# A decoder layer in one program: another buffer for the substitution's diagonal copy, another order around each group's boundary, and two engines that copy the solved rows

## The reference

```
def delta_rule(q, k, v, beta):                       # chunks of CS = 32 rows
    ...
    A = jnp.where(strict_lo, kb @ jnp.swapaxes(k, -1, -2), 0.0)
    Tinv = solve_triangular(eye + A, eye, lower=True, unit_diagonal=True)
    u = Tinv @ v
    w = Tinv @ kb
...
o = o * rsqrt(mean(o * o, -1) + 1e-05) * o_norm_w    # x = x + o @ o_proj_w.T
...
att = softmax(where(mask, q @ k.T / sqrt(16), -1e9))  # q from layernorm(x), k and v from the context
```

## Time and profile before

| | |
|---|---|
| median of 3 runs | 1211.49 us (1210.48 to 1219.17) |
| the profiled execution's own time | 1214.59 us |
| its span, from the first to the last instruction | 1212.8 us |
| mean granted clock of TensorE | 0.923 of full speed |
| busy share of the span | PE 85%, PEld 63%, DVE 68%, POOL 50%, ACT 44% |
| turns i = 0 to 7 of the loop, as stretches | 244.5 to 1004.0 us |

### The profile page before, as it was taken

One profiled execution on the slowest core, in us unless ns is written; L12 is line 12 of the kernel. 1 busy time (PEld: TensorE's weight loads), 2 busy tenths in 40 slices (PEclk: granted clock), 3 DMA queues, 4 the chain that ended last, 5 costly groups with the idle time before them and its releaser, 6 DMA issues.

```text
span 1212.8 us, 25582 instructions
## 1 busy us (share of the span) xinstructions
PE 1036.3 (85%) x9234; PEld 768.9 (63%) x9234; DVE 819.9 (68%) x2164; ACT 538.5 (44%) x1008; POOL 602.4 (50%) x998
## 2 busy tenths in 40 slices
PE   4899979486899899889989989979998898989982
PEld 2555558465677566666666656757666667767881
DVE  2989976834666756856766685684776765657576
ACT  3868754323334333432442433343243244754761
POOL 6877825147137346616806734651683124335552
PEclk9999999669799799989979989997998999999996
DMA  8365451530101511230161161121012064323588
GB/s 187 115 192 158 120 179 42 188 101 27 61 2 45 172 47 33 94 112 32 61 173 36 47 174 40 35 95 39 28 61 71 23 221 147 101 80 121 169 283 300
DMA packets 86796, 127.67 MB, mean 105 GB/s; under 512 B 28305, under 2 KB 62609, under 8 KB 84497
## 3 DMA queue, kind: packets, MB, share of 16 engines
q1 hardware_dynamic: 79472, 106.30, 29.1%
q0 software_dynamic: 7200, 19.74, 4.5%
HBM read 66.47 MB, written 59.55 MB: 104 GB/s over the span
## 4 chain that ended last, share of the span: by engine, by line
PE 44%; POOL 23%; DVE 16%; issue 8%; ACT 5%; DMA 3%; SPq 1%; ACTq 0%; DVEq 0%; POOLq 0%
POOL arena L1519 7%; POOL arena L1521 6%; PE bank L551 3%; PE bank L511 3%; POOL arena L1412 3%; PE bank L721 2%; PE bank L949 2%; PE bank L798 2%; PE bank L788 2%; PE bank L699 2%; POOL orn L1536 2%; PE bank L430 2%; PE bank L565 2%; PE bank L765 2%; PE bank L413 2%
## 5 line engine op out<-in xcount | busy, mean ns | idle before, releaser
L1023 ACT ACTIVATE arena<-bank 128x512 f32<-128x512 f32 (+4 forms) x374 | 195.9, 542 | 390.9 <-PE bank L940 65.1
L1642 DVE SCALAR_TENSOR_TENSOR arena<-arena,param 128x512 f32<-128x512 f32 x144 | 108.8, 767 | 16.1 <-ACT arena L1046 12.4
L1580 POOL DMA_INDIRECT results<-arena x78 | 76.6, 982 | 81.2 <-DVE arena L2190 51.2
L1519 POOL TENSOR_TENSOR arena<-arena 128x126 f32<-128x126 f32 (+22 forms) x217 | 91.5, 422 | 37.4 <-DVE arena L1738 21.9
L1483 POOL TENSOR_TENSOR arena<-arena,rb 128x256 f32<-128x256 f32 x32 | 19.9, 621 | 162.6 <-ACT arena L1023 162.2
L1521 POOL TENSOR_TENSOR arena<-arena 128x126 f32<-128x126 f32 (+22 forms) x217 | 87.0, 401 | 17.0
L413 PE MATMUL bank<-const,arena 128*128 128x128 f32 x256 | 42.5, 316 | 58.0 <-POOL arena L1412 26.1
L1829 DVE TENSOR_REDUCE top<-bank 128x8 f32<-128x512 f32 x64 | 43.9, 686 | 66.4 <-PE bank L568 66.3
L949 PE MATMUL bank<-arena 128*128 128x128 f32 x624 | 84.9, 280 | 0.2 <-ACT arena L1321 0.2
L1509 POOL COPY arena<-arena 32x128 f32<-32x128 f32 x128 | 50.9, 398 | 57.5 <-DVE arena L1728 50.9
L949 PEld LDWEIGHTS bank<-arena 128*128 128x128 f32 x624 | 78.2, 197 | 0.4 <-issue 0.4
(11 more groups left out here) (288 smaller groups left out, 2746.7 us busy)
## 6 DMA issues: line engine op xcount, KB each, us to landing
arena<-slots_x SPq DMA_DIRECT2D x78, 129.0 KB, 2.1
slots_x<-rows_of_no_token SPq DMA_DIRECT2D x8, 1161.0 KB, 11.5
xt<-x_in SPq DMA_DIRECT2D x16, 512.0 KB, 6.5
kq_T<-kq SPq DMA_DIRECT2D x8, 1024.0 KB, 4.4
kq<-kq_T SPq DMA_DIRECT2D x8, 1024.0 KB, 8.9
arena<-results SPq DMA_DIRECT2D x32, 256.0 KB, 5.2
arena<-ffn_in SPq DMA_DIRECT2D x7, 768.0 KB, 4.2
vT<-v_T SPq DMA_DIRECT2D x8, 514.0 KB, 5.0
```

The lines of the kernel that those rows point to most:

```text
L1023: free(act.activation(out_, in_, func, **kw), name)
L1519: own.link(pool.tensor_tensor(tmp, rows32[:, m0:, k].unsqueeze(2).broadcast_to([P, nm, k]), units[:, 0:k, k].unsqueeze(1).broadcast_to([P, ...
L1580: pool.indirect_dma_start(results[:, :], bass.IndirectOffsetOnAxis(ap=dest[:, n % YS:n % YS + 1], axis=0), ys[:, n % YS, :], None).then_in ...
L1642: ins = V.scalar_tensor_tensor(cv[:, k % 4, :], pre[:, j, d:d + GT], param[:, at + d:at + d + 1], cv[:, k % 4, :], ALU.mult, ALU.add)
```

## The change

- `Tn` moves from `NT` into `units`, the operand of the substitution, which is free once the blocks are solved. Its zero quarter is cleared by GpSimd after its last step (`upper_cleared`) and no more by VectorE. VectorE's `front_natural` is cut into a first transposition (needed by `pair_corner`), directly after `front_compact`, and a second (`front_second`, needed by `half_corner`) after the statistics. For group 0 both stand ahead of `long_turned`.
- On VectorE the sums and statistics come ahead of the second transposition and of `chosen`; `rows2` comes ahead of `masks`; `slots` and the last third of the short filter come after `queries`.
- On TensorE `pair_inner` stands between the two halves of the output projection; then come `pair_corner`, `context`, `half_inner`, `positions` (now in bank 7), the rows' transposition, the mask product. `masked_scores(1)` comes after the first tile of the recurrence instead of before it.
- Of the four solved tiles ScalarE copies the first two, VectorE the last two.

```
-        Tn = gflat[:, 0:HT * 2 * QB].rearrange("p (h c) -> p h c", h=HT)
+        Tn = units.rearrange("p j k -> p (j k)").rearrange("p (h c) -> p h c", h=HT)
 # TensorE, rows()
+                    pe.wait_ge(sem("x_rows_ready"), 2 * i + 1)
+                    transpose_rows(xn_x, [f"x1T0.{i}", f"x1T1.{i}"], (next(cross_bank), next(cross_bank)))
                     n = f"any.{i}"
                     o = open_bank(pe, n, next(cross_bank))
                     pe.wait_ge(sem("mask_ready"), i + 1)
                     full(mm(o[:, :], ones_b[0:S2, :], mT[:, :], start=True, stop=True), n)
-                    pe.wait_ge(sem("x_rows_ready"), 2 * i + 1)
-                    transpose_rows(xn_x, [f"x1T0.{i}", f"x1T1.{i}"], (next(cross_bank), next(cross_bank)))
 # TensorE, half_corner()
                 pe.wait_ge(sem("doubled"), 2 * i + 2)
+                pe.wait_ge(sem("natural_ready"), 2 * i + 2)
+                pe.wait_ge(sem("upper_cleared"), i + 1)
 # TensorE, body()
-                if i >= 2:
-                    positions(i - 2)
+                pair_corner(i)
                 if x:
                     context()
-                pair_corner(i)
+                half_inner(i)
+                if i >= 2:
+                    positions(i - 2, 7)
                 if x:
                     rows()
-                half_inner(i)
...
                 if x:
                     turned_scores(0)
-                    masked_scores(1)
...
+                    if x and t == 0:
+                        masked_scores(1)
...
                     full(last, n)
-                if ahead:
-                    pair_inner(i + 1)
+                    if ahead and k == 0:
+                        pair_inner(i + 1)
 # ScalarE
             def solved_rows(i):
-                for t in range(T):
+                for t in range(T // 2):
...
                 pair_corner(i)
+                half_inner(i)
                 if x:
                     rows()
-                half_inner(i)
 # GpSimd, end of front_steps()
+                done(pool.memset(Tn[0:QB, :, QB:], 0.0), "upper_cleared")
 # VectorE
             def front_natural(i):
                 dve.wait_ge(sem("compact_ready"), i + 1)
-                r = [slice(QB * q, QB * q + QB) for q in range(2)]
-                link(V.transpose(Tn[:, :, 0:QB], Tc))
-                V.memset(Tn[r[0], :, QB:], 0.0)
-                done(V.transpose(Tn[r[1], :, QB:], Tc[r[1], :, :]), "natural_ready")
+                done(V.transpose(Tn[:, :, 0:QB], Tc), "natural_ready")
+            def front_second(i):
+                dve.wait_ge(sem("natural_ready"), 2 * i + 1)
+                done(V.transpose(Tn[QB:2 * QB, :, QB:], Tc[QB:2 * QB, :, :]), "natural_ready")
...
+                    rows2()
                     masks()
-                    rows2()
-                    if i >= 2:
-                        slots(i - 2)
                     context()
                     anykey()
...
+                def solved_rows():
+                    for t in range(T // 2, T):
+                        n = f"solve{t}.{i}"
+                        o = filled(dve, n)
+                        free(V.tensor_copy(UW[:, t * H:(t + 1) * H, :], o[:, :].rearrange("p (h c) -> p h c", h=H)), n)
-                short_filter()
+                short_filter(range(FS - 1))
                 if x:
                     queries()
+                short_filter((FS - 1,))
+                if x:
+                    if i >= 2:
+                        slots(i - 2)
                     scores(0)
-                    scores(1)
+                    solved_rows()
                 else:
                     filled(dve, f"outer1.{i}")
                     for t in range(T):
                         front_gram(1, t)
+                    solved_rows()
                     front_units(1)
...
+                    if x and t == 0:
+                        scores(1)
...
                 if ahead:
                     front_compact(i + 1)
+                    front_natural(i + 1)
                 if x:
                     late_added()
-                if ahead:
-                    front_natural(i + 1)
-                if x:
-                    chosen(i - 1)
...
                 done(last, "x_stats_ready")
+                if ahead:
+                    front_second(i + 1)
+                if x:
+                    chosen(i - 1)
 # VectorE, ahead of the loop
             later_scales()
+            front_natural(0)
+            done(V.memset(Tn[0:QB, :, QB:], 0.0), "upper_cleared")
+            front_second(0)
             for c in range(CK):
                 long_turned(c)
...
-            front_natural(0)
```

14 lines of the change are left out of this document (7 added, 7 removed).

## The result

| | before | changed |
|---|---|---|
| median | 1213.05 us (4 runs, 1210.48 to 1219.17) | 1168.59 us (4 runs, 1165.83 to 1174.84) |
| the profiled execution, its span | 1214.59, 1212.8 us | 1165.83, 1164.0 us |
| mean granted clock | 0.923 | 0.945 |

The ratio is 0.9634 (95% interval 0.9579 to 0.9688): 3.7% faster. The forecast was 1162 with 1146 to 1190. A turn came to 92.7 (even) and 91.9 us (odd), where the prediction had 93 to 96.

The account below looks back on a forecast made before the run. A turn was taken as TensorE's work (91.8 of 101.6 us), its 10 us standing still, and the low clock. 4.5 + 0.6 + 3 x (2.0 + 2.3 + 1.6) + 3 x (6.8 + 2.3) = 50.1 gave 1162 us, range 1146 to 1190.

Parts of the forecast that it names:

- The forecast's case: Boundaries of turns: the clock still falls in even turns, no longer in odd ones; 50.1 us gained, chance 0.43.
- even boundary: Even turns, projection to queries' end: queries end at 626.0 instead of 627.99 with the clock low, gain 2.0 us a turn.
- odd boundary: Odd turns, projection to queries' end: full clock, queries from 719.4 to 723.1, gain 6.8 us a turn.
- behind the queries, even (2.3 + 1.6): Even turns after the queries: 2.3 us wait before second scores goes, and the second low clock stretch, 1.6 us.
- behind the queries, odd: Odd turns after the queries: the wait before the second scores goes, 2.3 us a turn.
- first turns: Ahead of the loop 4.5 us from VectorE's wait for the first group's products (lower end 0); turn 1 gains 0.6.
- last boundary: Boundary after the last turn, followed by the experts: the prediction gave no term for it.
- VectorE's side: Even boundary on VectorE: second sum starts at 611.1 instead of 612.42, deviations hide inside 1.7 us of work, rows at 616.3.
- if the clock falls at the corner, as it did: Even boundary: 1.2 GHz from the corner through the queries, `half_inner` 3.67 us, gain 2.0 instead of 6.2 us.
- The second scores: Moved behind the recurrence's first tile, copies shared by two engines: TensorE's 2.30 us wait goes in turns 2 to 7.
- rival 3: Another wait replaces it (values' load 2 us late, VectorE's copies, or filter): 12 to 24 us lost, 1173 to 1185, chance 0.11.
- Rival 1: The clock falls nowhere, in even or odd boundaries: gain 62.7 us, 1148.8 us, chance 0.18.

Follow-up runs that it names:

- run 12: The changed kernel again, unaltered, on the same chip as run 11: median of 6 runs 1166.01 us, ratio to the kernel before 0.9614.
- Run 4: Against the changed kernel, VectorE's second transposition and counts stand ahead of the sums and statistics again: 1165.17 us.
- run 3: Against the changed kernel, `pair_inner` stands behind both halves of the output projection again: 1192.98 us.
- run 8: Against the changed kernel, `half_inner` and its copies stand behind the places, the rows' transposition and the mask product again: 1193.29 us.
- run 2: Against the changed kernel, eight 128x128 and four 128x256 spare products on TensorE between corner and `half_inner` in turns 2, 4 and 6: 1167.55 us.
- run 5: Against the changed kernel, four 128x128 and two 128x256 spare products per even turn, half as many as in run 2: 1172.77 us.
- run 6: Against the changed kernel, the second tile's scores stand ahead of the recurrence's first tile again, solved rows still copied by two engines: 1179.45 us.
- run 7: Against the changed kernel, ScalarE copies all four solved tiles again, second scores staying behind the first tile: 1180.36 us.
- run 11: Changed kernel plus counts before sums at the last boundary, run 5's spare products, and even turns' last filter third before VectorE's queries: median 1160.02 us, ratio to before 0.9563.
- run 10: Against the changed kernel, the first group's turned copy stands behind `long_turned` again ahead of the loop: 1166.36 us.
- run 9: Against the kernel before, one edit alone: `pair_inner` between the two halves of the output projection: 1216.03 us.
- run 1: Against the changed kernel, the counts stand ahead of the sums on VectorE again at the last boundary only: 1163.59 us.

## Why the prediction was right

The forecast's case is the one that came: the clock falls in even turns and not in odd ones. Its sum was 50.1 us against 48.8 in the spans, but this closeness is partly luck, since three terms were mis-sized and nearly cancel (by the medians the gain is 44.5):

| term | forecast | measured |
|---|---|---|
| even boundary | 2.0 a turn | 3.7 to 3.8 |
| odd boundary | 6.8 a turn | 6.6 to 6.7 |
| behind the queries, even (2.3 + 1.6) | 3.9 a turn | 3.9 to 4.1 |
| behind the queries, odd | 2.3 a turn | 2.5, 2.5, 1.7 |
| turns 2 to 7 | 45.0 | 50.06 |
| first turns | 5.1 | 3.08 in the first profile, 0.25 in run 12's |
| last boundary | nothing | 4.34 lost |

- **VectorE's side** went by its steps: second sum and rows within 0.2 us of their forecast times. Run 4 corrects the credit: with `pair_inner` inside the projection the second sum waits for TensorE anyway, so that the order of sums and counts is worth at most 0.3 us a turn. Runs 3 and 8 show that the places of `pair_inner` and `half_inner` carry the boundary. What the early first transposition, the rows ahead of the masks and the mask product behind the transposition give by themselves isn't shown: no run undoes one of them alone.
- **The even boundary** failed in the step "if the clock falls at the corner, as it did". It falls 9.4 to 9.9 us after the projection's start instead of 7.1, about at the end of `half_inner`, which takes 2.05 us instead of 3.67. Runs 3 and 8 show that in even turns this hangs on the order of TensorE's list. With `pair_inner` put back TensorE has only 32x32 products and gaps for 3.6 us, with `half_inner` put back it stands still for 2.7 us; `half_inner` then runs at half clock, the low stretch lasts 10.3 to 13.7 us instead of 6.9, and 19.6 and 22.6 us are lost in turns 2 to 7. The prediction gave `pair_inner`'s move a cost (the projection ends 1.8 us later) and no benefit.
- **The odd boundary** went as forecast, and for the reason given in part: the granted clock is 1.00 throughout. But the context's products are not sufficient for it. In runs 2, 5, 6, 7 and 11 the clock fell in some odd turns whose instructions are in the changed kernel's order at that place, in run 7 in all three.
- **The second scores**: the wait of 2.30 us is gone, and runs 6 and 7 show that each edit alone would leave 0.8 to 1.0 of it. The second low stretch of even turns went with it; that the wait caused that stretch was inferred from its place, and isn't shown. Odd turns had the same wait of 2.30 us and no such stretch before, and in run 9, with the wait in all of them, it moved to the odd ones.
- **First turns**: the mechanism was right (the wait of 4.56 us gone, 3.9 to 5.4 us in that stage by run 10), the size in the whole isn't settled, because the first stage alone varies by more. Turn 1, forecast 0.6 shorter, is 1.07 longer in one profile and 1.7 shorter in run 12's (92.14), by whether the clock is low through its whole projection (9.31 us) or only in part (6.59).
- **What was missed**: the counts moved behind the statistics in all turns, the last one too, where the experts' first rows wait for the places. The working followed `chosen` through the steady turn only.

Of the rivals, the load of the next values (rival 3) is close behind, and that it cost nothing was luck as far as the working goes. In turn 4 the load was issued 16.7 us after the projection's start before the change and is issued 20.7 us after it now, 4 us later and not about 1. With the 7.8 us of before, the values would have come 2 us after TensorE wants them (26.4). But the load took 4.0, so they landed at 24.6 as before (24.5). Runs 5 and 11 show the same in this turn: issued at 18.9 and 16.9, the load took 5.6 and 8.1 us and landed at 24.5 and 24.9. In turn 2 of run 5, 1.9 us sooner than the changed kernel at that point, it landed late and TensorE waited 1.46. Rival 1's condition, an even boundary without a fall, was met with spare products in runs 2, 5 and 11, where that boundary gained 5.5 us over before in runs 5 and 11 and 3.7 to 4.3 in run 2, against 6.2 forecast. It didn't lower the sum of the turns: the spare products' own time, the wait for the values, and the clock, which then fell elsewhere, took it back.

The Trainium skill (TensorE: Matmul & The Clock Gate, "Part 1: The HAM clock gate") says that activity releases the throttle. The even boundaries of runs 2, 5 and 11, nine with a granted clock of 1.00 against three with a fall in the changed kernel's profile, agree. The odd boundaries agree with it in part only: they fell or held with the same work ahead of them, as the last section shows.

## What to carry to other kernels

Where TensorE is nearly the bound, price a move by what it does to the clock as well: two reorderings that only filled gaps were each worth some 20 us of 1165 in turns 2 to 7 (runs 3 and 8), and one of them was worth 2 in the kernel before, where another engine still held the rows back (run 9). Follow every moved step also through the turns that differ from the steady one, above all the last, where its consumers are others. A change that makes a stage sooner calls for a look at the loads that were just in time.

## What had not been expected of the hardware

- A low clock that is filled away in one place can turn up in another: with spare products even boundaries held 1.00 nine times of nine, and run 11's turns 2 to 7 still sum to 545.55 us against 545.62.
- The fall of the clock isn't set by TensorE's instructions at the place alone. Odd boundaries with the same order held in all three turns of the changed kernel and of runs 1, 4, 10 and 12, and fell in one of three in runs 2, 5, 6 and 11 and in three of three in run 7. It isn't only the order that was the same. These are the first 11.8 us of the boundary in turn 5 of the changed kernel, where the clock held, then in turn 7 of run 5, where it fell directly behind them, and the stretch of the fall:

```profile
678.35:690.15 11.80, 10.84 (x228) 9.25 (x227) 10.21 (x32) 7.15 (x13) 1.46 (x3) 1.00 0.38 129
```

```profile
865.62:877.42 11.80, 10.84 (x228) 9.26 (x227) 10.21 (x32) 7.14 (x13) 1.46 (x3) 1.00 0.27 90
877.42:884.20 6.78, 6.59 (x15) 3.41 (x15) 5.21 (x12) 1.19 (x2) 0.00 (x0) 0.50 0.01 2
```

  The busy times of all engines ahead of the fall agree within 0.01 us. Loads don't decide it either: the DMA share is 0.01 in this fall, 1.11 in the fall of run 7's turn 3 (505.7 to 512.5 us), and 1.10 at the same place of the changed kernel's turn 5, where the clock is 1.00.
- The same holds at the end of a turn. Ahead of the next projection TensorE waits 1.7 us for VectorE in turns 2 to 6 of the changed kernel, all of which held, and of run 11; in run 11 the clock fell behind that wait in turn 2 (the first row, at half clock) and in turn 4, and held in turn 6 (the second row):

```profile
489.12 1.91 PE L413 MATMUL bank<-const,arena 128*128 128x128 f32 x8 [1.73 <-DVE arena L2153]
...
857.08 1.09 PE L413 MATMUL bank<-const,arena 128*128 128x128 f32 x8 [1.72 <-DVE arena L2153]
```

  What decides between a fall and none at equal work stays open. The moment at which the boundary comes, and what ran long before it, were not separated.
